# A nine-product burst, b2's row through TensorE, and other loads and orders in a conditioned residual layer

## What is computed

```python
# x: (64, 128, 1024), cond: (64, 512), W3: (512, 1024), W2: (1024, 1024), float32
q_emb = relu(cond @ W3 + b3)
v_sum = sum(x, axis=1, keepdims=True)
y = (128 * x + v_sum) * q_emb[:, None, :]
out = x + relu(y @ W2 + b2)
```

## Time and profile before

| | before |
|---|---|
| time, median of 3 runs | 636.22 us (636.18 to 636.4) |
| the profiled execution | 635.75 us |
| its span, first to last instruction | 634.0 us |
| PE busy in the span | 629.2 us (99%) |
| DVE, ACT, POOL busy | 444.1, 418.9, 16.5 us |
| first product with W2 starts | 13.09 us |
| unbroken run of products | from 45.63 us |
| last result (DVE) starts | 630.77 us |

### The profile page before, as it was taken

The page is one execution under the profiler, slowest core; times in us unless marked ns, Lnnn a source line. Parts: engine busy times, 40 slices in busy tenths (PEclk is TensorE's granted clock), DMA queues, the critical chain, the costliest instruction groups (busy, mean ns, idle before and its releaser), DMA issues.

```text
span 634.0 us, 9260 instructions
## 1 busy us (share of the span) xinstructions
PE 629.2 (99%) x2795; PEld 518.4 (82%) x2796; DVE 444.1 (70%) x675; ACT 418.9 (66%) x897; POOL 16.5 (3%) x21
## 2 busy tenths in 40 slices
PE   9999999999999999999999999999999999999997
PEld 6888888888888888888888888888888888888886
DVE  3989979576776757677576776757677576776533
ACT  4879886839577594856839577494866839577320
POOL 2340000000000000000000000000000000000000
PEclk9999999999999999999999999999999999999999
DMA  8935736454353734436353353733346353350703
GB/s 301 400 138 196 264 136 227 173 197 143 141 182 132 256 141 135 137 158 232 132 199 137 139 187 132 255 142 131 134 165 232 132 199 132 144 189 0 259 6 132
DMA packets 26656, 108.83 MB, mean 172 GB/s; under 512 B 2961, under 2 KB 3089, under 8 KB 22802
## 3 DMA queue, kind: packets, MB, share of 16 engines
q1 hardware_dynamic: 26496, 108.54, 47.9%
q10 hardware_dynamic: 146, 0.14, 0.1%
HBM read 75.11 MB, written 33.55 MB: 171 GB/s over the span
## 4 chain that ended last, share of the span: by engine, by line
PE 92%; DVE 2%; issue 0%; POOL 0%; ACT 0%; DVEq 0%
PE acc L285 92%; DVE vsum L597 1%; DVE w_lo L678 1%; DVE scale L603 0%; DVE a_lo L662 0%; POOL x_sb L572 0%; DVE xn L686 0%; ACT a_hi L386 0%; DVE bias L605 0%; DVEq L691 0%
## 5 line engine op out<-in xcount | busy, mean ns | idle before, releaser
L285 PE MATMUL acc<-w_hi,a_hi 128*128 128x512 f32 x904 | 352.2, 390 | 0.2
L285 PE MATMUL acc<-w_lo,a_hi 128*128 128x512 f32 x904 | 351.7, 389 | 0.0
L285 PE MATMUL acc<-w_hi,a_lo 128*128 128x512 f32 x904 | 351.7, 389 | 0.0
L404 ACT ACTIVATE x_sb<-x_sb,bias,scale 128x128 f32<-128x128 f32 x492 | 203.2, 486 | 9.6 <-DVE bias L605 9.5
L285 PEld LDWEIGHTS acc<-w_hi,a_hi 128*128 128x128 f32 x904 | 169.7, 188 | 36.7 <-DVE a_lo L662 1.0
L285 PEld LDWEIGHTS acc<-w_hi,a_lo 128*128 128x128 f32 x904 | 169.7, 188 | 35.4
L285 PEld LDWEIGHTS acc<-w_lo,a_hi 128*128 128x128 f32 x904 | 169.7, 188 | 35.0
L673 DVE TENSOR_TENSOR a_lo<-x_sb,a_hi 128x512 fp32r<-128x512 f32 x150 | 103.5, 690 | 106.9 <-ACT a_hi L399 106.2
L399 ACT CAST a_hi<-x_sb 128x512 fp32r<-128x512 f32 x150 | 93.3, 622 | 39.5 <-PE acc L285 38.1
L399 ACT CAST a_hi<-s 128x512 fp32r<-128x512 f32 x60 | 37.4, 623 | 74.0 <-PE acc L285 69.1
L597 DVE TENSOR_REDUCE vsum<-x_sb 128x16 f32<-128x2048 f32 (+1 forms) x38 | 73.7, 1943 | 6.9 <-DMA x_sb<-x_t 6.7
(11 more groups left out here) (49 smaller groups left out, 192.9 us busy)
## 6 DMA issues: line engine op xcount, KB each, us to landing
xn<-x SPq DMA_DIRECT2D x64, 512.0 KB, 4.0
out<-xn SPq DMA_DIRECT2D x62, 512.0 KB, 3.2
x_sb<-x_t SPq DMA_DIRECT2D x30, 1024.0 KB, 5.1
x_sb<-w_t SPq DMA_DIRECT2D x4, 512.0 KB, 6.1
x_sb<-x_t SPq DMA_DIRECT2D x8, 256.0 KB, 11.7
u_sb<-w_q SPq DMA_DIRECT2D x3, 512.0 KB, 8.0
m_sb<-w_q SPq DMA_DIRECT2D x3, 512.0 KB, 7.6
w_stage<-w_q SPq DMA_DIRECT2D x2, 512.0 KB, 9.0
```

What stands on the lines that cost most here:

```text
L285: return nc.tensor.matmul(dst, lhs, rhs, start=False, stop=False, skip_group_check=True)
L404: last = nc.scalar.activation(x_sb[:, slot, t, k], x_sb[:, slot, t, k], ACT.Identity, bias=bias[:, slot, t, k:k + 1], scale=scale[:, slot, ...
```

## The change

It changes the start and the end of the program. The burst has nine products. The six zero products between the sums and the full-precision row product go; in their place the row of b2 is split into a high part (cast by ACT) and a low part (DVE), and six products of one row of ones with these parts seed banks 3, 2 and 4. ACT no longer seeds banks 2 and 4. Sums 6 and 7 move ahead of the second quarter of the first product; on ACT their `q_relu` stands ahead of the casts of pieces 2 and 3 of b11. The first half of b11 is loaded as two pieces of 256 KB, x block 2 moves ahead of its second half, and `b_first` behind blocks 3 and 4. DVE takes the scaling of block 7 and the difference `b_step - b_first` from POOL, and the order of its list changes. In the first pair after the plain one, ACT seeds banks 6 and 7 two steps earlier. At the end the last 512 columns are made in four parts, stored by SP and ACT in turn.

```diff
-    SEEDED = (2, 4, 5, 6, 7, 0, 1)
+    ROWS = (3, 2, 4)
+    SEEDED = (5, 6, 7, 0, 1)
+        row_hi = a_hi[0:1, 6].rearrange("p k n -> p (k n)")
+        row_lo = a_lo[0:1, 6].rearrange("p k n -> p (k n)")
+        row_ones = a_hi[0:1, 3, 0]
 # SP
+            def load_b11(k):
+                sp.dma_start(w_stage[:, k], w2_q[0, 0, :, k * MH:(k + 1) * MH]).then_inc(b11_first[k], 16)
             load_w3(2)
-            load_half(w_halves, 0, 0, 0, b11_loaded)
+            load_b11(0)
             load_w3(3)
+            load_b11(1)
+            load_first(2)
             load_half(w_halves, 0, 0, 1, b11_loaded)
-            load_first(2)
-            load_b(b_first, 0, b_first_loaded)
             for n in (3, 4):
                 load_first(n)
+            load_b(b_first, 0, b_first_loaded)
...
+            for c in range(2):
+                sp.wait_ge(c22_done, 2 * p + c + 1)
+                sp.dma_start(out[2 * (2 * p + c) + 1, :, MH:], xn[:, c, 1, MH:]).then_inc(tail_stored, 16)
+            sp.wait_ge(c21_done, 2 * p + 1)
+            sp.dma_start(out[2 * (2 * p) + 1, :, :MH], xn[:, 0, 1, :MH]).then_inc(tail_stored, 16)
+            for n in (0, 2):
+                part = slice(n * MH // 4, (n + 1) * MH // 4)
+                sp.wait_ge(part_done, n + 1)
+                sp.dma_start(out[2 * (2 * p + 1) + 1, :, part], xn[:, 1, 1, part]).then_inc(tail_stored, 16)
...
+            sp.wait_ge(tail_stored, 80)
+            sp.wait_ge(last_stored, 32)
 # PE
+            def b_row_part(n, part):
+                return add(acc[:, ROWS[n]], row_ones, part)
-            keep_warm(4)
+            add(acc[:, 2], warm[:, :P], warm[:])
             pe.wait_ge(small_loaded, 16)
             for k in range(KT - 2):
                 q_sum(k)
-                if k == KH - 1:
-                    pe.wait_ge(ones_set, 1)
-                    pe.wait_ge(row_loaded, 16)
-                    add(acc[:, 3], ones[:], b_row)
-                last = keep_warm(1)
-            last.then_inc(marked, 1)
+                if k == 1:
+                    pe.wait_ge(row_hi_ready, 1)
+                    b_row_part(0, row_hi)
+                if k == 2:
+                    pe.wait_ge(row_lo_ready, 1)
+                    b_row_part(0, row_lo)
+                if k == 3:
+                    b_row_part(1, row_hi)
+                if k == 4:
+                    b_row_part(1, row_lo)
+                    b_row_part(2, row_hi)
+            b_row_part(2, row_lo).then_inc(marked, 1)
...
-                    if n == 0 and k == KH // 2:
+                    if n == 0 and k == 1:
                         q_sum(KT - 2)
                         q_sum(KT - 1)
+                    if n == 0 and k == KH // 2:
                         pe.wait_ge(lo_ready, 1)
 # ACT
+            act.wait_ge(ones_set, 1)
+            nc.scalar.copy(row_ones, ones[:])
+            act.wait_ge(row_loaded, 16)
+            nc.scalar.copy(row_hi, b_row).then_inc(row_hi_ready, 1)
             act.wait_ge(small_loaded, 16)
             for k in range(KH):
                 q_relu(k)
             cast_first_half(0)
-            cast_w("b11", 0, b11_loaded[0], 16)
+            cast_w("b11", 0, b11_first[0], 16)
             cast_first_half(1)
-            cast_w("b11", 1, b11_loaded[0], 16)
             for k in (4, 5):
                 q_relu(k)
-            for k in range(2, W_PIECES):
-                cast_w("b11", k, b11_loaded[k // 2], 16)
-            cast_first(1)
+            cast_w("b11", 1, b11_first[1], 16)
             for k in (6, 7):
                 q_relu(k)
-            act.wait_ge(marked, 1)
-            act.wait_ge(b_first_loaded, 16)
-            seed_plain(2, b_first)
+            for k in range(2, W_PIECES):
+                cast_w("b11", k, b11_loaded[1], 16)
+            cast_first(1)
             scale_first(2)
             cast_first(2)
             act.wait_ge(q_ready, KT)
-            for bank in (4, 5):
-                seed_plain(bank, b_first)
+            act.wait_ge(marked, 1)
+            act.wait_ge(b_first_loaded, 16)
+            seed_plain(5, b_first)
...
-                    if i in (5, 6):
+                    if first and i in (3, 4):
+                        seed_r(p, i - 3)
+                    if i in (5, 6) and not first:
                         seed_r(p, i - 5)
...
+            for n in (1, 3):
+                part = slice(n * MH // 4, (n + 1) * MH // 4)
+                act.wait_ge(part_done, n + 1)
+                act.dma_start(out[B - 1, :, part], xn[:, 1, 1, part]).then_inc(last_stored, 16)
 # POOL
-            for n in (1, 4, 7):
+            for n in (1, 4):
                 scale_first(n)
-            pool.wait_ge(b_seeded, len(SEEDED))
-            nc.gpsimd.tensor_tensor(b_step[:], b_step[:], b_first[:], ALU.subtract).then_inc(b_step_ready, 1)
 # DVE
+            dve.wait_ge(row_hi_ready, 1)
+            nc.vector.tensor_tensor(row_lo, b_row, row_hi.bitcast(fp32), ALU.subtract).then_inc(row_lo_ready, 1)
...
-            for k in range(1, W_PIECES):
-                low_w("b11", k)
+            low_w("b11", 1)
             sums_0(2)
             scalars_0(2)
+            for k in range(2, W_PIECES):
+                low_w("b11", k)
             low_first(1)
             sums_0(3)
             scalars_0(3)
+            scale_first(3)
+            low_first(2)
             sums_0(4)
-            low_first(2)
             scalars_0(4)
-            scale_first(3)
+            low_first(3)
+            low_w("b21", 0)
             sums_0(5)
             scalars_0(5)
-            low_first(3)
-            low_w("b21", 0)
             low_first(4)
             low_w("b21", 1)
             sums_0(6)
...
             scalars_0(7)
+            scale_first(7)
+            low_first(6)
...
+            dve.wait_ge(b_seeded, len(SEEDED))
+            nc.vector.tensor_tensor(b_step[:], b_step[:], b_first[:], ALU.subtract).then_inc(b_step_ready, 1)
+            low_w("b22", 0)
             low_first(8)
+            low_w("b22", 1)
...
+            c21(p, 1, 0)
+            dve.wait_ge(prod_done, done_by(p, 4, 1))
+            for n in range(4):
+                part = slice(n * MH // 4, (n + 1) * MH // 4)
+                o = xn[:, 1, 1, part]
+                nc.vector.scalar_tensor_tensor(o, p_bank(1, 1)[:, part], 0.0, o, ALU.max, ALU.add).then_inc(part_done, 1)
```

More of the change, by code:

```diff
@@ L98, in cond_residual @@
         small_loaded, row_loaded, ones_set = sem("small_loaded"), sem("row_loaded"), sem("ones_set")
+        row_hi_ready, row_lo_ready = sem("row_hi_ready"), sem("row_lo_ready")
         b_first_loaded, b_step_loaded = sem("b_first_loaded"), sem("b_step_loaded")
@@ L102, in cond_residual @@
         x1_loaded = [sem(f"x1_loaded{c}") for c in range(2)]
+        b11_first = [sem(f"b11_first{k}") for k in range(2)]
         b11_loaded = [sem(f"b11_loaded{h}") for h in range(2)]
@@ L110, in cond_residual @@
         stored = [[sem(f"stored{c}{t}") for t in range(2)] for c in range(2)]
-        tail_stored = sem("tail_stored")
+        tail_stored, part_done, last_stored = sem("tail_stored"), sem("part_done"), sem("last_stored")
         table_set, warm_set = sem("table_set"), sem("warm_set")
@@ L279, in _ @@
                 sp.wait_ge(stored[c][1], 16 * (PAIRS - 1))
-            sp.wait_ge(tail_stored, 64)
+            sp.wait_ge(tail_stored, 80)
+            sp.wait_ge(last_stored, 32)
         @block.tensor
@@ L758, in _ @@
             scalars_0(7)
+            scale_first(7)
+            low_first(6)
             dve.wait_ge(w_lo_ready, split("b11", W_PIECES - 1))
[L761 to L765, removed]
+            for h in range(2):
+                dve.wait_ge(b12_loaded[h], 16)
+                w_sum(w_halves, v_halves, w_halves, h, t1_ready)
             low_first(7)
@@ L772, in _ @@
                 scalars_usual(1, 1, c)
-            for h in range(2):
-                low_w("b22", h)
+            dve.wait_ge(b_seeded, len(SEEDED))
+            nc.vector.tensor_tensor(b_step[:], b_step[:], b_first[:], ALU.subtract).then_inc(b_step_ready, 1)
+            low_w("b22", 0)
             low_first(8)
+            low_w("b22", 1)
             plain_result(4, 0, 0, 0, c11_done)
@@ L844, in _ @@
                 c12(p, c)
-            for c in range(2):
-                c21(p, 1, c)
+            c21(p, 1, 0)
[4 more added lines that the diff above has]
+                nc.vector.scalar_tensor_tensor(o, p_bank(1, 1)[:, part], 0.0, o, ALU.max, ALU.add).then_inc(part_done, 1)
 def kernel(x, cond_1024, L0_cond_W3, L0_cond_b3, L0_cond_W2, L0_cond_b2):
```

## The result

The changed kernel takes 643.84 us (median of 5 executions, 641.94 to 644.22), the kernel before beside it 636.18 us: ratio 1.0119, 95% interval 1.0102 to 1.0135. It is slower by 7.7 us, and the time lies outside the range of 635.0 to 637.2. The profiled execution took 644.22 us, with a span of 642.4 and a mean granted clock of 0.986, where the kernel before had 634.0 and 1.000.

The account below looks back on a forecast made before the run. The prediction took TensorE, busy for 99% of the span, to bound the kernel. Start and middle netted 0.0 us and the end -0.2, giving 636.0 us against a median of 636.22, with a range of 635.0 to 637.2.

Parts of the forecast that it names:

- rival B: New early holes make TensorE's clock fall, most likely at 15.7 to 16.9 us: 1.6 us later, 637.6; chance 0.07.
- A row product at 0.2268: Ahead of sum 3's end: two row products take 0.45 in place of 0.73 us, so sum 3 ends 0.28 earlier.
- The burst, worth 0: Program start: three zero products fewer gain 0, at most 0.05 us, and open a hole of 0.6 us.
- rival C: The row of b2, taken to land at 5.7, lands late and holds all q_relu: 1 us per us past 6.4; chance 0.07.
- First product at 12.64: First product of W2 starts at 12.64 in place of 13.09, through an earlier b11 load and shorter sums.
- The hole of 1.2 us from ScalarE's order: Ahead of the third quarter: q_relu 6 and 7 before the b11 casts leave TensorE idle from 15.7 to 16.9.
- Third quarter at first product + 4.26: Third quarter of the first W2 product starts at 16.90, after a start at 12.64; before the change it was 16.45.
- GpSimd's scaling 4: Scaling of block 4, beside VectorE's work, takes over 3 us and ends between 23.5 and 25.3: cost 0 to 0.3, taken 0.15.
- No hole at 45.63: Before the long unbroken run of products: the wait for block 8's low part closes, cost 0.
- The end, -0.2: Last 512 columns made and stored in four parts: net 0.27 us won, up to 0.5 lost if stores queue; taken -0.2.
- The sum: Whole kernel: 0.0 up to TensorE's long run and -0.2 at the end give -0.2 us, 636.0 us.

Follow-up runs that it names:

- tall rows: Changed kernel with row products made over 128 partitions, the other 127 rows zero: 636.19 us with a burst of twelve, 635.87 with nine.
- both put back: Changed kernel with the burst of twelve and a full zero product behind each of the first six sums: 637.84, 638.47, 638.86 and 641.63 us, ratio 1.0054.

## Why the prediction was wrong, point by point

- **The clock (rival B).** The step that failed is the first sentence on the row products, that they "have the shape 512 columns of the W2 products". They have its columns and 1 of its 128 rows. I asked of every hole whether it would let the clock fall and never of the products that took the zeros' place whether they would hold it. The clock fell where TensorE had no hole at all, near 10.4, two holes before the place I had named. The low stretch was 16.7 us long where I priced 3.4: the length of the first low stretch, which I had used as a measure, said nothing of this one. The chance of 0.07 and the price of 1.6 were both far too small: 8.0 us lie between the changed kernel and the one with tall rows (spans 642.4 and 634.4). At full clock a one-row product costs 0.34 more than a tall one with the sum beside it (1.46 against 1.12), so by my estimate at most 2 of the 8.0 are the six products themselves, and the rest is the clock.
- **A row product at 0.2268.** 0.42 at full clock with one row, 0.32 with 128 (7.50 to 7.82), of which 0.1 is the step from one kind of product to the other. From the start of sum 0 to the end of sum 3 the kernel before takes 4.09 us, and I forecast 3.81. It is 3.95 with tall rows (5.80 to 9.75), half of the gain, and 4.74 with one-row products at full clock (burst twelve put back, 5.96 to 10.70).
- **The burst, worth 0.** Right in the middle (635.88 with nine against 636.12), wrong in the spread: three of ten executions of the kernel before with nine lose 6 to 8 us. I looked at one execution, in which the clock rose at 4.6, and took that time for a property of the kernel. In other profiles it rose near 7.1 (tall rows with ScalarE's order back, burst of twelve), near 7.0 (the changed kernel) and after 30 us (the profile of the version with zeros put back). The hole of 0.6 behind the burst was not there: sum 0 started at 5.05.
- **The row of b2 lands at 5.7 (rival C).** It was in at 5.0; ScalarE's cast of it started at 5.02. Right.
- **First product at 12.64.** 12.88 in the version with tall rows and a burst of nine, and 13.15 with twelve. With nine it was the load: I had the first 256 KB of b11 in at 10.9 and the wait for it gone, they were in at 11.27, and the cast started at 11.29. With twelve it was the sums, which began only at 5.80.
- **The hole of 1.2 us from ScalarE's order.** Right: 1.37 between the starts at 16.17 and 17.54, 1.14 of it lost. It is also the one step that the runs show to be worth undoing: 1.5 us between the medians of "both put back" with and without it (from four executions on one side, one of them with a clock that fell; the hole accounts for 1.1), 0.6 and 0.3 with tall rows, where something else came next.
- **Third quarter at first product + 4.26.** 4.39 and 4.40, so it stood at 17.54 and 17.28 where I had 16.90.
- **GpSimd's scaling 4.** "Over 3 us": 3.30, to 25.33, the upper bound of my range for its end. It made nobody late, since the third quarter was late already.
- **No hole at 45.63.** Right, in the changed kernel and in the tall one: 2706 products follow each other from the third quarter to the end, 613.62 us in the tall one, 0.2268 each.
- **The end, -0.2.** 0.0 by the medians, but the interval of that run reaches from 0.7 us less to 0.5 us more and does not exclude my 0.2. The traces are finer: from the start of the last results to the end of the span it is 3.15 to 3.23 us in the profiles with the new end, against 3.23, where I had 3.0. So 0.1 at the most.
- **The sum.** -0.2, 636.0, is met by the kernel in which the row products are tall: 636.19 with twelve, 635.87 with nine. So nearly all of the miss is one assumption about the products in the zeros' place. That the total agrees to 0.2 is in part luck. The profiled spans, 634.4 and 634.1 against 634.0 before, are 0.4 and 0.1 longer where I had 0.2 less, since the third quarter was 0.4 to 0.6 late and the end gave 0.1 at the most.

## What to carry to other kernels

Products that keep TensorE's clock up are load-bearing even when their result is zero: whoever takes them out has to try on the chip whether what comes in their place keeps the clock, for a TensorE that stays busy with one-row products lost it here. A useful product of one row can be made over all 128 partitions with zeros in the others, at the price of a few memsets on an idle engine, and then does both jobs: in 43 executions of four kernels with such rows none was over 636.8 us. And a warm-up has to be judged over many executions: one profile shows one moment of the clock's rise, and the shorter burst looked free in the median.

## What the runs showed of the hardware

- Same instruction count, same columns, same order, 1 partition in place of 128 in six products: the clock falls to 1.2 GHz for about 10 us, and the kernel takes 6.0 us more (642.10 against 636.12). Fewer records go through in the stretch before the fall (39 against 43 from 5 to 11 us), so whether the rows or the stream count is not shown.
- TensorE can be busy in every microsecond by its row in the profile and still lose its clock: 5.40 of 5.40 us up to the fall in the changed kernel, and no weight load waited over 0.65 us between 5.1 and 17.5 us. The Trainium skill (TensorE: Matmul & The Clock Gate, Part 1) says that the clock follows how busy the engine has been. By these runs the busy time of the profile does not tell it: with six products of 1 partition in place of 128 it is 6.00 of 6.00 us from 5 to 11 us, where the kernel before has 5.84, and the clock is lost right behind.
- The weight load behind a one-row product comes late: 0.42 us after the product's start (7.58 to 8.00), with the loads idle for 0.24 us. Behind a product over 128 partitions it comes 0.09 us after the start:

```profile
7.47 0.19 PEld L308 LDWEIGHTS acc<-a_hi 128*128 128x128 f32 x1
7.59 1.09 PEld L308 LDWEIGHTS acc<-small_sb,x_sb 128*128 128x128 f32 x8
```

- Until the clock first changes in a trace, the granted clock column reads 1.00 whatever it is: 85 records in 25 us, W2 products 0.43 us apart, shown as 1.00. In the first microseconds only the spacing tells.
